# Two small-head attentions on one Trainium2 core: value blocks grouped in runs, the sum copied one slot sooner, and the first stacks filled during an earlier stage

## What is computed

```python
x = x + _L0_xattn_ref(_layernorm(x), ctx_2048, w_qkv, w_proj, b_proj)   # 16 heads of 8
x = x + _L0_ffn_ref(...)
x = x + _L1_xattn_ref(ctx_2048, _layernorm(x), mask_BxS2_ik0, b)        # 8 heads of 16
...
# each: softmax(q k^T * scale) v, for every batch and head; the first one's keys are
# the 1601 context rows and the 256 own rows, the second one's the 1601 context rows, masked
```

## Time and profile before

| what | us |
|---|---|
| median of 3 runs | 4348.81 (4346.71 to 4349.35) |
| the profiled execution's own time | 4352.28 |
| its span, first to last instruction | 4350.5 |
| `cross0`: up to the attention's block | 0 to 155 |
| attention of `cross0`: POOL fills the stacks, loads | 155 to 200 |
| attention of `cross0`: at work | 200 to 918 |
| attention of `cross1`: POOL fills the stacks, loads | 1220 to 1284 |
| attention of `cross1`: at work | 1284 to 1656 |

### The profile page before, as it was taken

The page is one execution under the profiler, slowest core; times in us unless marked ns, Lnnn a source line. Parts: engine busy times, 40 slices in busy tenths (PEclk is TensorE's granted clock), DMA queues, the critical chain, the costliest instruction groups (busy, mean ns, idle before and its releaser), DMA issues. The chain is left out here.

```text
span 4350.5 us, 72117 instructions
## 1 busy us (share of the span) xinstructions
PE 3715.5 (85%) x28012; PEld 2215.1 (51%) x28017; DVE 2957.8 (68%) x4910; ACT 2293.6 (53%) x3860; POOL 1545.0 (36%) x1271
## 2 busy tenths in 40 slices
PE   2299999989819998699779999999999999999654
PEld 2133333358704443467446666666666666666441
DVE  3399999944428883655337777777777777777747
ACT  3188888853307775122226666565666565656330
POOL 0300000000040010421007766667666667776410
PEclk6589999989959998799889999999999999999877
DMA  5222222100035530100010000000000000000000
GB/s 175 66 45 42 49 51 49 36 12 23 12 66 88 82 60 2 30 2 2 9 61 1 16 1 16 1 16 1 16 1 16 1 16 1 1 1 1 7 30 24
DMA packets 117717, 122.89 MB, mean 28 GB/s; under 512 B 19008, under 2 KB 95649, under 8 KB 116993
## 3 DMA queue, kind: packets, MB, share of 16 engines
q1 hardware_dynamic: 117240, 117.84, 12.4%
q10 hardware_dynamic: 144, 0.52, 0.0%
HBM read 102.51 MB, written 15.68 MB: 27 GB/s over the span
## 5 line engine op out<-in xcount | busy, mean ns | idle before, releaser
L814 DVE TENSOR_REDUCE att_peak.1<-psS 128x1 f32<-128x512 f32 (+1 forms) x1024 | 580.8, 633 | 93.7 <-PE psS L691 93.4
L2156 POOL TENSOR_TENSOR key_sums_0.1<-key_sums_0.1,prob_0.1 128x512 f32<-128x512 f32 x256 | 440.4, 1720 | 28.7 <-POOL key_sums_0.1 L2156 0.4
L2156 POOL TENSOR_TENSOR key_sums_1.1<-key_sums_1.1,prob_1.1 128x512 f32<-128x512 f32 x256 | 421.1, 1645 | 28.7 <-POOL key_sums_1.1 L2151 0.4
L786 ACT ACTIVATE att_probT.1<-psT 128x512 f32<-128x512 f32 (+1 forms) x682 | 368.8, 568 | 75.1 <-PE psT L720 33.8
L2065 DVE TENSOR_TENSOR att_highest.1<-att_highest.1,prob_0.1 128x1024 f32<-128x1024 f32 (+1 forms) x160 | 273.3, 1708 | 128.1 <-ACT prob_0.1 L2000 121.5
L2065 DVE TENSOR_TENSOR att_highest.1<-att_highest.1,prob_1.1 128x1024 f32<-128x1024 f32 (+1 forms) x160 | 278.7, 1742 | 114.7 <-ACT prob_1.1 L2000 107.5
L691 PE MATMUL psS<-key_stack.1,query_stack.1 64*128 64x512 bf16 (+1 forms) x1024 | 272.1, 387 | 93.5 <-DMA key_stack.1<-key_parts 47.2
L814 DVE TENSOR_REDUCE att_peak.2<-psS 128x1 f32<-128x512 f32 (+1 forms) x512 | 265.8, 568 | 114.7 <-PE psS L691 113.6
L737 PE MATMUL psM<-att_probT.1,quad_values.1 128*9 128x256 f32 (+1 forms) x3840 | 305.9, 391 | 19.4 <-issue 19.4
L2086 DVE TENSOR_TENSOR prob_0.1<-prob_0.1,psO 128x1024 f32<-128x1024 f32 (+1 forms) x256 | 243.9, 1015 | 49.0 <-PE psO L1916 49.0
L2086 DVE TENSOR_TENSOR prob_1.1<-prob_1.1,psO 128x1024 f32<-128x1024 f32 (+1 forms) x256 | 243.9, 1015 | 49.1 <-PE psO L1916 49.1
(11 more groups left out here) (690 smaller groups left out, 7985.6 us busy)
## 6 DMA issues: line engine op xcount, KB each, us to landing
key_stack.1<-key_parts SPq DMA_DIRECT2D x384, 58.0 KB
key_stack.2<-key_parts SPq DMA_DIRECT2D x96, 200.1 KB
ctx_rows.1<-in_ctx_dram SPq DMA_DIRECT2D x8, 1536.0 KB
key_parts<-split_parts.1 SPq DMA_DIRECT2D x8, 1200.8 KB, 5.7
ctx_keys_0.1<-in_ctx_dram SPq DMA_DIRECT2D x4, 768.0 KB
ctx_keys_1.1<-in_ctx_dram SPq DMA_DIRECT2D x4, 768.0 KB
query_stack.1<-query_parts SPq DMA_DIRECT2D x192, 16.0 KB
ctx_values_0.1<-in_ctx_dram SPq DMA_DIRECT2D x4, 768.0 KB
```

Of the source, the lines that this page charges most:

```text
L786: self.k.nc.scalar.activation(probs[:, blks[0]:blks[-1] + 1, :].rearrange("p b q -> p (b q)"), bank[0:w, 0:len(blks) * S], ACT.Exp).then_i ...
L814: self.k.nc.vector.tensor_reduce(self.peak[:, 2 * h + s, c:c + 1], self.score_bank[m % 3][:, 0:w], AX_X, ALU.max).then_inc(self.peak_done. ...
L2156: nc.gpsimd.tensor_tensor(acc, acc, own[:, h, c * BANK:(c + 1) * BANK], ALU.add).then_inc(self.summed.sem, 1)
```

## The change

It does five things. The context split gets a POOL program, `att.pool_prepare`, so the stacks of `cross0` are filled there; their tiles are allocated before the split and the rest later (`open`). The first load of queries goes from SP's queue to ACT's, in both attentions. The table `VALUE_RUNS` groups the value blocks: a run stands in every second slot (0, 2, 4, 6 of the even pair, 0, 2, 4 of the odd one), of two blocks, with one run of three in `cross0` (blocks 8 to 10) and one of a single block in `cross1`. ACT copies psM one slot sooner. In `cross1` the stacks are filled where they were.

```diff
-def split_context(k):
+def split_context(k, prepare):
...
+        @block.gpsimd
+        def _(pool):
+            prepare(pool)
...
+    VALUE_RUNS = {15: [(0, 2), (2, 4), (4, 6), (6, 8), (8, 11), (11, 13), (13, 15)],
+                  13: [(0, 2), (2, 4), (4, 6), (6, 7), (7, 9), (9, 11), (11, 13)]}
...
     def sp_run(self, sp, crows):
...
-            if q % 2 == 0:
+            if q % 2 == 0 and q > 0:
                 self.load_queries(sp, q // 2)
...
     def pool_run(self, pool, crows, own=None):
-        self.pool_prepare(pool)
...
     def pe_run(self, pe):
-        half = -(-self.NK // 2)
+        runs = self.VALUE_RUNS[self.NK]
...
-                blk = half * odd + i
-                if 0 <= q - 1 < self.quads and i < half and blk < self.NK:
-                    self.pe_values(pe, q - 1, blk)
+                if 0 <= q - 1 < self.quads and i % 2 == 0 and 4 * odd + i // 2 < len(runs):
+                    for blk in range(*runs[4 * odd + i // 2]):
+                        self.pe_values(pe, q - 1, blk)
...
     def act_run(self, act):
+        act.wait_ge(*self.zeroed(self.zeroings))
+        self.load_queries(act, 0)
...
-                if i == self.NB - 1 and odd and 0 <= q - 1 < self.quads:
+                if i == self.NB - 2 and odd and 0 <= q - 1 < self.quads:
                     self.act_partial(act, q - 1)
...
-    split_context(k)
...
+        att = PairedAttention(k, mem, chunks, blocks, bins, hd, H, halves=True)
+        split_context(k, att.pool_prepare)
...
+            att.open(own)
```

More of the change, by code:

```diff
@@ L457, with __init__ @@
                    7: [[(1, 3), (1, 4)], [(1, 5)], [(1, 6)], [(1, 7)], [(2, 0)], [(2, 1)], [(2, 2)]]}
-    def __init__(self, k, mem, chunks, blocks, bins, hd, heads, halves, masked=False):
+    VALUE_RUNS = {15: [(0, 2), (2, 4), (4, 6), (6, 8), (8, 11), (11, 13), (13, 15)],
+                  13: [(0, 2), (2, 4), (4, 6), (6, 7), (7, 9), (9, 11), (11, 13)]}
+    def __init__(self, k, early, chunks, blocks, bins, hd, heads, halves, masked=False):
         self.k, self.chunks, self.blocks, self.bins, self.hd, self.heads = k, chunks, blocks, bins, hd, heads
@@ L469, in __init__ @@
         lanes = [] if halves else [2]
[L470 to L479, removed]
+        self.key_stack = sb("key_stack", [P, self.RING, 2, *lanes, self.width], BF16, ctx=early)
+        self.query_stack = sb("query_stack", [P, 2, 4, *lanes, S], BF16, ctx=early)
+        self.ident = sb("ident_bf16", [P, P], BF16, ctx=early)
+        self.vquad = sb("quad_values", [P, 2, self.NK, 4, hd + 1], ctx=early)
         self.score_bank = [k.psS[:, n, :] for n in range(3)]
@@ L494, in __init__, with open @@
         self.ctx_loaded = [k.flag(f"ctx_loaded_{i}") for i in range(2)]
+    def open(self, mem):
+        sb = self.k.sb
+        self.peak = sb("att_peak", [P, 4, self.NC], ctx=mem)
+        self.shift = sb("att_shift", [P, 4], ctx=mem)
+        self.shift_parts = sb("att_shift_parts", [P, 4, 3], BF16, ctx=mem)
+        self.probT = sb("att_probT", [P, self.RING, 2, self.NK, S], ctx=mem)
+        self.sums = sb("att_sums", [P, S], ctx=mem)
+        self.rtotal = sb("att_rtotal", [P, 2, 4], ctx=mem)
     def finish(self):
@@ L859, in cross0 @@
     NKEY = KC + S
-    split_context(k)
+    chunks = [(0, 512), (512, 512), (1024, 512), (1536, KTAIL + S)]
+    blocks = [(t * P, P) for t in range(KB - 1)] + [((KB - 1) * P, KTAIL), (KC, P), (KC + P, P)]
+    bins = [(t, t + 1) for t in range(0, KB - 1, 2)] + [(KB - 1,), (KB, KB + 1)]
     own_done, own_copied = k.flag("value_done"), k.flag("value_copied")
@@ L899, in cross0 @@
         own_copied.passed(1)
-        chunks = [(0, 512), (512, 512), (1024, 512), (1536, KTAIL + S)]
-        blocks = [(t * P, P) for t in range(KB - 1)] + [((KB - 1) * P, KTAIL), (KC, P), (KC + P, P)]
-        bins = [(t, t + 1) for t in range(0, KB - 1, 2)] + [(KB - 1,), (KB, KB + 1)]
         with ExitStack() as own:
             crows = [k.sb(f"ctx_values_{i}", [P, KB, D], ctx=own) for i in range(2)]
-            att = PairedAttention(k, own, chunks, blocks, bins, hd, H, halves=True)
+            att.open(own)
             block = own.enter_context(nc.Block())
@@ L1011, in cross1 @@
         att = PairedAttention(k, mem, chunks, blocks, bins, hd, H, halves=False, masked=True)
+        att.open(mem)
         block = mem.enter_context(nc.Block())
@@ L1019, in _ @@
         def _(pool):
+            att.pool_prepare(pool)
             att.pool_run(pool, crows)
```

## The result

| | before | after |
|---|---|---|
| median, us | 4349.1 (4346.7 to 4352.1, 4 runs) | 4387.9 (4385.7 to 4392.2, 4 runs) |
| profiled execution's own time, us | 4352.28 | 4392.23 |
| its span, us | 4350.5 | 4390.5 |

The ratio is 1.0091, with a 95% interval of 1.0076 to 1.0106: slower by 0.9%. The forecast was 4351 us, the range 4318 to 4372; the kernel came out 16 us beyond its upper end.

The account below looks back on a forecast made before the run. DVE was taken to bound cross0's quads (busy 19.95 of 21.93 us), PE cross1's (20.95 of 22.40). 4352.3 - 35.3 + 0.5 - 4.5 + 51 - 10 gave 4354 us, 4351 as median; range 4318 to 4372.

Parts of the forecast that it names:

- The ring's working: cross0's three score banks: 1.66 us in hand against 1.87 for a run of two; DVE starved 2.1 us a quad.
- 22.6 us: A cross0 quad of the changed kernel at full clock, against 21.34 us now.
- 19.95 + 2.1 to 19.95 + 2.7: A cross0 quad at full clock: DVE's busy time of 19.95 us plus 2.1 to 2.7 us of starving.
- I take 22 of 30: cross0 quads with a fall of PE's clock, 1.39 us each, 1.0 us a quad; 12 of 29 now.
- +51: Cost of runs and earlier copy in cross0: 23.6 us a quad against 21.93, over 30 quads, in us.
- The queries on ACT's queue: Query loads leave SP's queue, so keys come 4.1 us earlier in cross0; in cross1 4.5 us, between 2 and 5.7.
- 0.7 us of the 2.4: Gain taken per cross1 quad from runs and earlier copy, of 2.4 us at most; 15 quads, -10 us.
- The seams' saving of 1.26 us of PE: cross1: a run saves PE 0.21 us for each block joining another, six of thirteen a quad.
- The memsets beside the split: POOL's 31 us of memsets beside the context split: cost taken as 0.5 us, between nothing and 7.3.
- The earlier copy takes away the wait for it, which is in these figures: cross0 quad: the sooner copy of the sums ends the wait for it, counted within the 22.6 us.
- the first rival: cross0: the clock falls no oftener than now, +38 us, 4338; with none, +20 us, 4320; chance 0.27.
- the bound from above, +62 us: cross0: a clock fall in each quad, 24.0 us a quad, +62 us.

Follow-up runs that it names:

- 10: Experiment 4 with one run of two in cross0: block 3 moved from slot 3 to slot 2 of the even pair; 4279.7 us.
- 11: Experiment 4 with one run of two in cross0: block 7 moved from slot 7 to slot 6 of the even pair; 4267.7 us.
- experiment 12: Experiment 4 with runs of two in slots 0, 2, 4 and 6 of cross0's even pair, odd pair left in single blocks; 4292.9 us.
- 2: The kernel before with only ACT's copy of the sums one slot sooner; 4297.6 us.
- experiment 4: The changed kernel with values one block to a slot, early filling, earlier copy and queries on ACT's queue kept; 4263.1 us.
- 7: Experiment 4 with the first queries back on SP's queue ahead of the keys, in both attentions; 4266.2 us.
- 8: Experiment 7 with PE's turn of the sums in cross0 in slot 4 instead of 1, DVE's division in slot 5; 4263.5 us.
- 9: Experiment 8 with the first queries of cross1 alone on ACT's queue; 4260.7 us.
- 1: The changed kernel with values one block to a slot and the copy in the last slot, as before; 4319.5 us.
- 6: The changed kernel with the three runs of cross0's odd pair one slot later, in slots 1, 3 and 5; 4378.2 us.
- 3: The changed kernel with ACT's copy of the sums back in the last slot; 4437.1 us.
- Experiment 5: The changed kernel with each transposed score in slots 5 to 7 of cross0's odd pair computed twice; 4373.9 us.

## Why the prediction was wrong

*The mechanism stands in the main.* The ring's working was right for a single run, 0.43 us in slot 2 and 0 in slot 6 [experiments 10, 11], and for the sum of the even pair's, 0.69 [experiment 12], though not for its terms one by one. In the changed kernel DVE's waits behind the odd pair's first two runs are 0.56 and 0.57 us, where I had 0.56 and 0.41, and none shows behind the third. For the clock, the longest stretch from one value block's start to the next orders most of the kernels: 3.2 us, no fall (2, 4, 7 to 12); 3.9 us, 12 and 13 quads of 29 (before, 1); 4.4 to 4.7 us, eleven quads with 21 falls (6); 5.9 us and more, every quad (the changed kernel, 3). Experiment 5 doesn't fit the order: 6.1 us and more in nearly every quad, with more work for PE in them, and 15 of 29 with a fall. A single fall costs 1.33 to 1.39 us. Four terms were mis-sized, and none of the errors cancelled another. From the forecast 4354 for the profiled execution:

1. **"22.6 us" for a quad at full clock.** The nearest thing measured is 22.97, with the odd pair's runs one slot later. Of this 21.50 is the quad with the even pair's runs (0.69 of it as forecast); the odd pair's runs cost 1.47 us there, where I had 0.56 + 0.41 + 0.13 = 1.10. The idle part was sized well: I had put "19.95 + 2.1 to 19.95 + 2.7" and taken 2.65, and it is 22.97 - 20.26 = 2.71. What failed is the floor of 19.95, taken as fixed. It is 20.26 in experiment 6, 0.31 more, since DVE's shift and POOL's copies and memsets now run side by side and the shift lengthens by as much. In the changed kernel's own windows the floor is 20.36 and 20.42, of which the shift is 0.25. No run takes the overlap away with the runs left, so its effect on the time and on the falls is not measured. Some 0.37 x 30 = 11 us.
2. **"I take 22 of 30" falls.** There was one in each of 29, of twice the length in the four longest. 24.33 - 22.97 = 1.36 us a quad, where I had 1.0: another 11 us, if the changed kernel's quad at full clock is that of experiment 6. The emptier stretch is 5.9 to 6.3 us and not 5.3. These two are 22 of the 24 us between +51 and +75.
3. **The queries on ACT's queue.** Forecast: 4.1 us earlier in `cross0`. Shown by the traces: later, by 3.0 us in the changed kernel against 7, by 2.1 in the mean of all. They became the transfer that ends last. ACT's twelve issues cost nothing, as said, but from the last of them (158.3) to the first score are 12.0 us; SP meanwhile issues keys and the first batch of values. That the values' bulk holds the queries up is argued, not tried. In `cross1` the move gives 2.5 us, of "4.5". The start of `cross0`: -31.2 - 1.5 (its block begins at 153.9, a time that moved between 151.9 and 155.7 from trace to trace) + 3.0 = -29.7.
4. **"0.7 us of the 2.4" in cross1.** It was 0.38. Taken apart, the copy gives 1.07 (22.43 to 21.36) and the runs lose 0.69. The seams' saving of 1.26 us of PE is not to be seen: PE is busy for 21.05 us a quad with runs and 20.90 with single blocks. Windows of a quad, the changed kernel and that of experiment 4:

```profile
1378.30:1400.30 22.00, 21.05 (x200) 9.54 (x199) 18.22 (x44) 15.77 (x33) 2.00 (x4) 1.00 0.50 77
```

```profile
1267.10:1288.45 21.35, 20.90 (x200) 9.21 (x199) 18.60 (x44) 15.85 (x34) 2.04 (x5) 1.00 0.54 79
```

Where it went is open.

So 4354 + 5.1 (start) + 24.2 + 2.9 + 5.2 + 0.9 = 4392, the profiled time.

*The memsets beside the split* cost nothing that shows: the two-input step lasts 1.83 us with POOL filling beside it, at 23.93 and at 30.36, as alone:

```profile
23.93 1.83 DVE L434 TENSOR_TENSOR split_parts.1<-split_rest.1,split_parts.1 128x1601 bf16<-128x1601 f32 x1 [1.59 <-ACT split_parts.1 L423]
```

The Trainium skill's rule on the shared interface ("GPSIMD Engine Reference", section 1, Specifications), weighed in the prediction, does not show in the split. The Trainium skill's page "SBUF — State Buffer" (section "Who interferes with whom") adds that a DVE instruction with two SBUF inputs contends with a GpSimd instruction that reads SBUF and not with one that only writes it; a memset reads none, and with that the trace agrees. It agrees in the attention, too, where I hadn't looked: there the two-input step beside POOL's copy takes 0.45 us in place of 0.16 [experiment 6].

*The copy was never priced by itself.* "The earlier copy takes away the wait for it, which is in these figures" was true, and it hid the finding: 34 us of gain in `cross0` and 15 in `cross1`, together more than the two starts. The falls of before were explained by the length of the stretch; the first rival's doubt was that they "may have hung on" that wait. For the kernel before both readings are open, since the moved copy took away the wait and 0.7 us of the stretch at once. For the kernel after, the rival is wrong: the wait for the copy is gone and every quad has a fall.

*The range.* A fall in each quad was named as the bound from above, +62 us. It alone gives 4362 for the median (4351 + 62 - 51), inside the range. With every other term at the worse bound that the text gives too (-31.2, -2, +63 for 22.65 and a fall, 0 in `cross1`), but for the memsets, which cost nothing, it is 4352.3 + 29.8 - 3.5 = 4379, outside, and still 9 us below the measured time: 0.32 us a quad by which 22.65 was passed would be about as much. The range counted on errors of both signs; these all had one.

## What to carry to other kernels

Where one engine is three short buffers ahead of another, price each piece of foreign work by the slack at its own place: the same two blocks cost 0.43 us in one slot and nothing behind a 1.0 us operation of the consumer. With several such pieces the sum held here (0.71 us for a forecast of 0.69) and the places did not. Bundling saves seams only for an engine that is the bound, and here it took away the filling that kept TensorE's clock up; price the quad at half clock as well, since the bundle itself may then run slow (1.90 us in place of 1.05). The busy time of the engine that is the bound is no fixed floor: look at what the moved work sets off on its neighbours, and when. And cost each of several edits alone, even where they "belong together": here the starts and the copy together were worth 2% and the runs cost 3%.

## What the runs showed that was not expected

- The twelve falls of the kernel before went with one moved instruction: 21.93 to 20.79 us a quad, of which what goes at full clock is 21.34 - 20.79 = 0.55 and the falls 0.59.
- Falls can come in pairs: 25.7 us against 22.97 at a clock of 0.87, in ten of 29 quads, and then not at all for two quads.
- Twelve small query loads moved to a second queue, to run beside the keys, landed later than in front of them: 14.0 to 16.6 against 13.1 to 14.2 us to the first score; with larger keys (`cross1`) it was the reverse, 16.1 to 17.1 against 18.3 to 19.1.
- Work that ends earlier on PE let POOL start earlier, beside DVE's shift, and the shift grew from 0.86 to 1.11 and 1.17 us: the engine that was the bound was busy for 0.3 to 0.5 us more in each quad.
